# Two plane clears moved to the sync engine's queue, two adjacency row loads issued earlier among the scatters, and the first tile's scores written head by head

## The reference

```python
h = relu(layernorm(x))
# layer 0: 8 heads; only the first 1500 rows have related pairs (10000 of them)
q, k = h @ Wq.T + bq, h @ Wk.T + bk
scores[h, sub, obj] = (q[sub] * k[obj]).sum(-1) / 8      # at the pairs
scores elsewhere = -inf outside adj, 0 inside; diagonal 1e-7
x = x + softmax(scores).sum(heads) / 8 @ h
h = relu(layernorm(x))
# layer 1: 16 heads over all 2048 rows, masked by adj
x = x + elu(gat(h, adj) @ W_out + b_out)
```

## Time and profile before

| | us |
|---|---|
| median of 3 runs | 1203.23 |
| lowest and highest of them | 1200.37 to 1211.79 |
| the profiled execution | 1206.7 |
| its span in the trace | 1204.7 |
| PE busy in the span | 1100.0 (91%) |
| DVE busy | 951.7 (79%) |
| ACT busy | 806.5 (67%) |
| POOL busy | 124.5 (10%) |
| mean granted TensorE clock | 0.974 of full |

### The profile page before, as it was taken

One profiled execution on the slowest core, in us unless ns is written; L12 is line 12 of the kernel. 1 busy time (PEld: TensorE's weight loads), 2 busy tenths in 40 slices (PEclk: granted clock), 3 DMA queues, 4 the chain that ended last, 5 costly groups with the idle time before them and its releaser, 6 DMA issues.

```text
span 1204.7 us, 24632 instructions
## 1 busy us (share of the span) xinstructions
PE 1100.0 (91%) x10559; PEld 762.2 (63%) x10565; DVE 951.7 (79%) x1325; ACT 806.5 (67%) x843; POOL 124.5 (10%) x143
## 2 busy tenths in 40 slices
PE   4999576899999999999988699999999999999997
PEld 3444232344444444444444599999999999999843
DVE  2542415899999999998962899999999999999565
ACT  1343225566776666677533999999999999999022
POOL 2577750000000000000000000000000000000011
PEclk9999887999999999999999899999999999999999
DMA  9341244122212221010160310111100010101311
GB/s 348 109 36 37 72 85 99 37 64 64 59 38 49 46 64 55 35 36 18 38 237 35 114 38 37 42 63 42 37 37 38 37 37 38 37 37 37 107 70 70
DMA packets 35197, 77.69 MB, mean 64 GB/s; under 512 B 5653, under 2 KB 10642, under 8 KB 33042
## 3 DMA queue, kind: packets, MB, share of 16 engines
q1 hardware_dynamic: 27298, 60.55, 14.1%
q0 software_dynamic: 7792, 15.58, 7.3%
HBM read 65.39 MB, written 23.21 MB: 74 GB/s over the span
## 4 chain that ended last, share of the span: by engine, by line
PE 74%; DMA 7%; POOL 6%; issue 5%; ACT 5%; DVE 3%; SPq 0%; DVEq 0%; POOLq 0%; ACTq 0%
PE psum L1572 14%; PE psum L736 12%; PE psum L651 11%; PE psum L1569 8%; PE psum L1570 8%; PE psum L1573 7%; POOL rel_planes L152 5%; DMA rel_planes<-f_ones,f_flat 5%; PE psum L755 5%; PE psum L1667 5%; PE psum L706 2%; ACT area_b L946 2%; ACT area_h L1416 2%; DMA rel_planes<-f_h 1%; DVE area_b L1155 1%
## 5 line engine op out<-in xcount | busy, mean ns | idle before, releaser
L1416 ACT ACTIVATE area_h<-area_a,keep 128x2048 fp8e4<-128x2048 f32 x208 | 396.9, 1987 | 2.0 <-DMA area_a<-s_rows 2.0
L1572 PE MATMUL psum<-s_V,area_h 128*128 128x198 bf16 x2048 | 286.0, 249 | 0.0
L1573 PE MATMUL psum<-s_V,late 128*128 128x99 bf16 x2048 | 280.1, 209 | 0.0
L1569 PE MATMUL psum<-s_V,area_h 128*128 128x99 bf16 x2048 | 206.0, 210 | 11.6 <-DVE area_b L1471 11.0
L1570 PE MATMUL psum<-s_V,area_b 128*128 128x99 bf16 x2048 | 205.9, 209 | 0.0
L1572 PEld LDWEIGHTS psum<-s_V,area_h 128*128 128x128 fp8e4 x2048 | 199.6, 97 | 0.2
L1573 PEld LDWEIGHTS psum<-s_V,late 128*128 128x128 fp8e4 x2048 | 199.7, 97 | 0.0
L1569 PEld LDWEIGHTS psum<-s_V,area_h 128*128 128x128 fp8e4 x2048 | 189.5, 98 | 13.0 <-issue 11.9
L1570 PEld LDWEIGHTS psum<-s_V,area_b 128*128 128x128 fp8e4 x2048 | 189.6, 98 | 0.0
L1155 DVE CUSTOM_DVE_ANT_0 area_b<-psum,late 128x1500 f32<-128x1500 f32 x96 | 161.2, 1717 | 34.3 <-PE psum L651 31.6
L736 PE MATMUL psum<-area_h,f_region 128*128 128x512 f32 x384 | 181.7, 598 | 0.0
(11 more groups left out here) (172 smaller groups left out, 1163.4 us busy)
## 6 DMA issues: line engine op xcount, KB each, us to landing
area_a<-s_rows SPq DMA_DIRECT2D x16, 1024.0 KB, 4.5
rel_planes<-f_h POOLq DMA_DIRECT2D x3, 2304.0 KB, 16.2
late<-rel_planes SPq DMA_DIRECT2D x36, 192.0 KB, 2.5
area_h<-in_x SPq DMA_DIRECT2D x4, 1024.0 KB, 25.5
keep<-in_adj POOLq DMA_DIRECT2D x16, 256.0 KB, 5.8
f_region<-in_x SPq DMA_DIRECT2D x16, 256.0 KB, 2.6
x<-f_region SPq DMA_DIRECT2D x16, 256.0 KB, 2.0
area_a<-adj_chunks SPq DMA_DIRECT2D x4, 1024.0 KB, 9.5
```

The lines of the kernel that those rows point to most:

```text
L1416: act.activation(masks[:, j, :], s1b[:, b, :], ACT.Relu, bias=t["s2"][:, n, 0, j:j + 1], scale=BIG, saturate=False).then_inc(signs, 1)
L1569: pe.matmul(out[:, :, 0:DZ], masks[:, j, cols], V[:, b, j, :, 0:DZ], **first)
L1572: pe.matmul(out, masks[:, j, cols], V[:, b, j, :, :], **first)
L1573: last = pe.matmul(out[:, :, DZ:CZ], nadjT[:, NEAR_TILES.index(j), cols], V[:, b, j, :, DZ:CZ], **then)
```

## The change

Planes 1 and 2 are no longer cleared from POOL after `Wk`, but from SP, between `Wk` and `Wq`. SP waits for POOL's two first memsets before that. `PLANE` starts with three scatters into plane 0 and goes round through planes 1, 2, 0 from then on. The loads k = 5 and k = 6 stand after the scatters 56 and 72. In `front` the heads 2 to 7 of tile 0 are made by `score_head`.

```diff
-PLANE = (0,) * 4 + (1, 0) * 3 + tuple(i % PLANES for i in range(EC - 10))
-LATE_LOADS = {66: ADJ_RING, 76: ADJ_RING + 1}
+PLANE = (0,) * 3 + tuple((i + 1) % PLANES for i in range(EC - 3))
+LATE_LOADS = {56: ADJ_RING, 72: ADJ_RING + 1}
...
+    def clear_plane(self, queue, t, i):
+        queue.dma_start(t["rel_planes"][i].rearrange("(t p) j -> p t j", p=P),
+                        self.zero[:, None, :].bitcast(U8).to_broadcast([P, ET, NE])).then_inc(self.plane_zero[i], 16)
...
         load_w(K, "L0_gnn_Wk")
+        sp.wait_ge(zero_set, 2)
+        for i in range(1, PLANES):
+            f.clear_plane(sp, t, i)
         load_w(Q, "L0_gnn_Wq")
...
-        clear_plane(0)
+        f.clear_plane(pool, t, 0)
...
-        pool.wait_ge(w_in[K], 16)
-        for i in range(1, PLANES):
-            clear_plane(i)
         pool.wait_ge(flat_ready, 1)
         f.scatter(pool, t, 0, 10)
...
                 turn_h(1)
-                for p in range(1, PAIRS):
-                    score(0, p)
+                for hd in range(2, HA):
+                    score_head(0, hd)
```

More of the change, by code:

```diff
@@ L247, in gpsimd @@
         pool.wait_ge(zero_set, 2)
-        def clear_plane(i):
-            pool.dma_start(t["rel_planes"][i].rearrange("(t p) j -> p t j", p=P),
-                           zero[:, None, :].bitcast(U8).to_broadcast([P, ET, NE])).then_inc(f.plane_zero[i], 16)
-        clear_plane(0)
+        f.clear_plane(pool, t, 0)
         pool.memset(t["ident"][:, :], 0.0).then_inc(s["zeroed"], 1)
```

## The result

| | before | changed |
|---|---|---|
| median | 1206.2 (4 runs) | 1188.21 (4 runs) |
| lowest and highest | 1200.37 to 1211.79 | 1187.04 to 1189.33 |
| profiled execution, its span | 1206.7, 1204.7 | 1189.33, 1187.4 |
| row factors of tile 0 made at | 217.91 | 200.42 |
| from there to the end of the span | 986.8 | 987.0 |

The changed kernel takes 0.9851 of the time, with a 95% interval of 0.9814 to 0.9888: 1.5% faster, or 18.0 us of 1206.2. Two more comparisons on other chips, of six and five runs of the changed kernel, gave 0.9836 [0.9813, 0.9860] and 0.9828 [0.9813, 0.9843]. In the pair of profiled executions the whole gain of 17.3 (spans 1204.7 and 1187.4) lies ahead of the moment at which tile 0's row factors are made: 217.91 - 200.42 = 17.5.

The account below looks back on a forecast made before the run. The front up to tile 0's row factors (217.91) was taken as the bound: scatter start, row loads, scores. Gains 13.0 (6.0 loads, 7.0 clears) + 6 = 19 off 1206.7 give 1187.7; less 3.5, 1184.2, range 1174 to 1195.

Parts of the forecast that it names:

- The clears: Start of the scatters: clears on SP's queue let scatter 10 go at 45.2, 7.0 us ahead of 52.16.
- quick scatters: Rival, chance 0.20: a scatter takes 2.85 us beside SP's clears, scatter 10 some 12.6 ahead, total 1178.6.
- Behind scatter 10 both do the same per scatter, so 7 stays: Scatters after 10: one every 1.49 us in both programs, so the lead of 7.0 us stays.
- The late loads: Row loads k = 5 and 6 issued earlier: no wait for k = 5, k = 6 6.0 us earlier from its place.
- Wq: Wq loaded behind the clears: lands at 30.2 to 39.6, PE may lose 0 to 5 us, which is free.
- The slower rival: Rival, chance 0.04: SP's clears delay Wq so PE stands at 35.05; landing at 81.5 makes the time 1223.
- The scores: Tile 0's heads 2 to 7 made head by head, without waits on both earlier masks: gain 6 us, from 4.7 to 9.2.
- the one by DVE: Scores to row factors limited by six masks of 1.72 and joining for tile 1: 21.6 us, a gain of 5.8.
- head 2 at half clock and five at full: PE's clock in tile 0's scores: 5.3 + 13.6 = 18.9 us, then 22.7 to the factors, a gain of 4.7.
- overlap at the seams only: Scores on PE: only a head's last chunk runs beside the next head's first, 1.8 us off each of five heads.
- The half-clock rival: Rival, chance 0.08: PE's clock stays half during the scores, 35.7 us to the factors against 27.4, total 1198.5.
- The marks' margin of 0.7: Head 2's scores: loads allow 177.5, marks (first mask from 175.0) are done at 176.8, so loads decide by 0.7 us.

Follow-up runs that it names:

- `x` held back: Changed kernel with SP loading the last three quarters of x only after the third projection group, at 33.6 us: 0.9850 of the kernel before.
- the kernel without the heads: Changed kernel with the scores of tile 0 made in pairs again: 0.9867 of the kernel before.
- without the clears: Changed kernel with PLANE and the two clears on POOL's queue as before: 0.9933 of the kernel before.
- The runs with early loads: Changed kernel with load k = 6 behind scatter 64: 0.9842; with k = 5 behind 46 and k = 6 behind 66: 0.9836 of the kernel before.
- filler: Kernel with k = 5 behind 46 and k = 6 behind 66, plus fourteen unread matmuls ahead of head 2's scores: 0.9829 of the kernel before.

## Why the prediction was right, and where it was not

The forecast was 1184.2 in 1174 to 1195, and the median is 1188.2. Of the 4.0 between them 3.0 were in the starting point: I took the sum off the profiled 1206.7 and then set that 3.5 above the median of three runs, 1203.2. The medians of the next comparisons were 1206.2 to 1207.3. The profiled execution was the typical one. So the total came out well within the range; two of its three terms were off in opposite directions, which is luck and told below. Against 1206.7 the sum of 19 gives 1187.7, and the profiled execution of the changed kernel took 1189.3.

**Where the gain is cashed: right.** From the factors on it is 987.0, as forecast 986.8. Not everything in there is the same: the first two steps of twelve are 1.2 and 1.7 longer from factors to factors than before (35.86 and 36.85 against 34.62 and 35.15), and the eleventh interval is 1.7 shorter (34.47 against 36.17), with the rest of the program 1.1 shorter.

**The clears: the term was too small.** Forecast 7.0 at scatter 10; measured 9.1 there (43.03), 9.9 against the kernel that differs in the clears alone, and 11.7 of the whole by the medians. The step that failed is the price of a scatter beside SP's traffic. I took 6.6 from one row; it was 5.7 to 5.9, so scatter 2 went at 24.55 and not 24.9, scatter 3 at 30.58 and not 31.8, and scatter 6 at 36.63 and not 38.7. The chance of 0.20 for quick scatters is answered too: none of the three behind the clears took 2.85, and the quickest in any run took 4.2 at most, with `x` held back. The Trainium skill's two rules (DMA: Bandwidth & Descriptors, section Queues, rings and completion order) are both seen in part: a scatter did get through while SP's queue was full, and its completion still took twice the 2.85. No run takes the two rules apart.

**"Behind scatter 10 both do the same per scatter, so 7 stays": not so in this pair, and it cancelled the error before.** In the shown executions 108.1 pass from scatter 10 to 72 and not 106.0, so 9.1 became 7.0 at scatter 72. Thus k = 6 was issued at 152.34 where 152.35 was forecast: a right number from two wrong ones, by luck. The premise, one scatter every 1.49 from scatter 10 on, was a wrong reading: the 62 scatters from 10 to 72 took 106.0 before, 1.71 each, since POOL also issues the loads there and waits for landings. What in the edit lengthens this stretch is not shown. The likeliest is that PE, released early from k = 5, lets SP's next transfers go before scatter 72; about 1.7 of the 2.1 is the mean of all executions, and the rest, or more, is their spread.

**The late loads: 6.0 was too much.** The step that failed took the 6.0 that the table gives the load as arriving whole at S. By the medians the new place is worth 2.5 with the new clears (17.0 of 1206.5 against 19.5, the mean of the changed kernel's three ratios, on different chips) and 2.4 alone. By the trace k = 6 goes 3.6 to 4.5 earlier than in the kernel without this part (152.34, 151.91, 151.39 against 155.93; 5.6 in the kernel without the heads), not 6.0, and S is held by the marks soon after (below). PE's wait for k = 6 was 8.76, forecast 7, and there was none for k = 5. The load took 5.76 and not 5.25, so PE went on at 158.24 and not 157.6.

**Wq: right.** The slower rival needed a landing at 61.5. These are the issues of the first 40 us (KB each, median us to landing), for the earlier trace rows:

```profile
rel_planes<-f_h SPq DMA_DIRECT2D x2, 2304.0 KB, 22.8
...
late<-in_L_gnn_Wq SPq DMA_DIRECT2D x1, 1024.0 KB, 15.5
```

And SP's timeline:

```profile
15.38 5.53 SPq L239 DMA_DIRECT2D late<-in_L_gnn_Wq  x1
```

Issued at 15.38, Wq was there at 30.9, near the fast end of my 30.2 to 39.6, since the engines ran at about 400 GB/s all through. PE needed it at 36.01 and did not wait. It came to the rows of k = 5 at 137.4, 0.8 later than before (136.6), which was free.

**The scores: right in sum by the traces, wrong in how they get there.** S to F fell by 5.7 in the mean, where 6 was taken from 4.7 to 9.2; by the medians the part is worth 3.5 to 4.5. Of the three bounds the one by DVE fits: 21.6 forecast from S to F, 21.5 measured. DVE's masks run from 184.20 on, 5.3 behind S, with the joining for tile 1 between them; the joining took 2.6 and not 3.9, and DVE waited 1.4 for PE. But "head 2 at half clock and five at full" isn't what happened: in the shown execution the clock was 0.50, 0.78, 0.67 and only then 1.00, and in the second it was full from the start.

The overlap was wrong too. At half clock heads 2 and 3 alone in the array would take 10.6, with one shared chunk 8.9; they took 6.23, or some 7.4 if the last 1.2 us, which the trace grants full clock, are counted double. At full clock it would be 5.4 and 4.5, and they took 3.74. The Trainium skill (TensorE: Matmul & The Clock Gate, section The mechanism) let me expect overlap at the seams only; the traces differ, and they decide. The rows of two and five passes in equal windows show head 3 beside head 2 from its third pass on, four passes of six. It is so in ten of the eleven executions head by head, at either clock. In the eleventh, without the clears, head 3 starts at 188.02, when head 1's mask ends (187.96). The later heads start less early because they wait for their banks. Head 5 starts at 187.63, when the mask of head 3 ends (185.85 + 1.72 = 187.57), with three passes beside head 4; head 7 starts at 193.78, when that of head 5 ends (192.00 + 1.72 = 193.72), with two beside head 6. So DVE's masks set the overlap there, and not the order on PE. Why a head may start two chunks before the one ahead of it is through was not tried. The half-clock rival would have given 35.7 from S to F; the longest that any run head by head took was 22.9.

**The marks' margin of 0.7: too thin to be a statement.** In the three executions S followed the first mask by 2.5 to 3.3, so the loads did decide, by 0.7 to 1.5 beyond the one mask of 1.78. The runs with early loads show what that means: past this margin scatter 80 sets the pace, and no place of the loads that was tried brings it forward beyond the spread: 10 to 80 took 119.5 to 122.6 in every kernel run here (119.0 in the one before).

## What to carry to other kernels

Where two chains end within a few us of each other, taking a wait off one of them is worth no more than the margin; here two further edits of the loads' place, each of which took away PE's last wait for a load, gave nothing. When an engine is released early, look up which transfers will now go early and what they stand in front of: here some two of the six us of an edit were lost between two scatters, probably to that, and the loss was hidden in a number that came out right. Take the price of a small DMA beside a full queue from a row of the same queue state, and let the sum start from the profiled time and end there, since three runs' median can lie 3 us off.

## What the runs showed of the hardware that was not expected

A scatter of 125 bytes took 5.7 to 5.9 us while SP's queue moved clears, weights and `x` at about 400 GB/s, and at most 4.2 when the same queue ran dry halfway; with the clears ahead of it in its own queue it had taken 18.05. Six passes of one head and six of the next, in different halves of the array, overlapped by four passes, at half clock (6.23 us in the changed kernel) and at full (3.74 in its second execution), wherever the second head didn't have to wait for its banks. The clock granted at one place differs between executions of one program: 0.50, 1.00 and 0.77 in the first 1.8 us of head 2's scores in three executions of the changed kernel. And with PE kept busy by filler for 5.5 of 7.9 us ahead of them, the scores' window was granted 0.60 of full clock, where it was granted 0.66 with an idle PE ahead.
